# A fused transformer block on one core: attention probabilities of chunks 8 to 11 weighed in one run at the next group's first chunk, where chunks 8 and 9 had a run of their own

## The chip, the cores and the metric

The kernel runs on one core of a Trainium2 chip. Its time is the device time of one execution in microseconds (us), as the median of several executions.

## What is computed

The reference is one transformer block in float32 with a shift, scale and gate per batch entry: a causal attention with 16 heads of 32 and then a mixture of 32 experts with a shared expert. Only the attention matters here:

```python
B, S, D_MODEL, N_HEADS, D_K = 8, 1024, 512, 16, 32
q, k, v = proj(w_q, b_q), proj(w_k, b_k), proj(w_v, b_v)
scores = einsum('bhqd,bhkd->bhqk', q, k) / sqrt(D_K)
scores = where(causal, scores, -inf)
attn = softmax(scores, axis=-1)
out = einsum('bhqk,bhkd->bqhd', attn, v)
x = x + ga * (out @ w_o.T + b_o)
h = layernorm(x) * (1 + cb) + sb
x = x + gb * (routed experts(h) + shared expert(h))
```

## The kernel before, in words

The program has four stages on one core, one after the other: the projections to queries, keys and values (lines with the tile prefix qkv_), the attention (att_), the output projection with the shared expert (ffn_) and the routed experts (exp_). Work is handed between the engines by semaphores, and the order of each engine's work is written out by hand.

**Groups and chunks.** The attention works on 32 groups (GROUPS), each of one batch entry and four heads (GH = 4). The keys lie on the partitions: a chunk is one tile of 128 keys against one half of 512 queries, for the four heads. A group has 12 chunks, in the order of the list `chunks`. Chunks 0 to 3 belong to the first half of the queries, 4 to 11 to the second. A chunk on the causal diagonal has fewer queries: chunks 8 and 9 have 512 a head, chunk 10 has 256 and chunk 11 has 128. `heads_each` puts several narrow heads into one bank, so a chunk is 4, 2 or 1 "problems" (chunk 10 has two, chunk 11 one).

**The loop of TensorE** is `step` in `tensor`, once per group `prev` (the next group is `cur`). For each problem it computes the transposed scores into one of three banks `ps_p` (line 1385; on the diagonal line 1388 adds a mask), and lets ScalarE know. Between them it computes pieces of the plain scores of the next group into four banks `ps_s` (`scores`, line 1303; `TILES` says how many behind each problem; from chunk 9 on they are those of the group after next). VectorE takes the row maxima from these (`maxima`, lines 247 and 253) so that the softmax can subtract them: at chunk 9 they are turned (line 1367), VectorE writes `m_hi` and `m_lo` (lines 266 and 268), and SyncE copies both into a row each of the next group's queries (`load_maxima`, line 236). TensorE waits for those two copies (`m_in`) before the next group's chunk 0.

**Exponentials.** ScalarE turns each problem's bank into probabilities in a tile `pt` (lines 1165 and 1168). There are 9 tiles for 12 chunks (`PT`), so a chunk's first exponential waits in `tile_free` until the tile's former user has been weighed (`pv_done`) and its sum taken. GpSimd adds chunks' tiles together for the sums of the softmax (`join`, lines 1097 to 1104), and TensorE adds the rest with ones (`total`, line 1360; in the last group `last_total`, line 1337).

**Weighing** (`weigh`, line 1329) multiplies a chunk's probabilities with the values: for each of the four heads a matmul with 128x32 weights, whose result takes 32 of the 128 partitions of the bank `ps_o`. In the trace each of these matmuls is two instructions, so a chunk is 8. `step` weighs two chunks at a time, after the last problem of each even chunk c:

```python
                    group = prev if c else older(prev)
                    if group and c % 2 == 0:
                        weigh(group, (c - 2) % NC)
                        weigh(group, (c - 1) % NC)
```

So chunks 8 and 9 are weighed at chunk 10, and chunks 10 and 11 at chunk 0 of the next group. ScalarE takes the finished half out of the bank (`take`, line 1122) at chunk 1.

**The end of the stage.** In the last group there are no plain scores. Its sums are computed chunk by chunk with ones; behind the loop come the sums and then the weighing of chunks 10 and 11. ScalarE meanwhile has the last exponential, five copies of weights (lines 1180 and 1185), with `take_total(end, 1)` (line 1128) ahead of the last of them, and then `take(end, NC - 1)`. The next stage's first transpose on TensorE (line 2209) waits for `t_free`, which that `take_total` gives; its ScalarE work waits behind `take`. SyncE and GpSimd start their part of the next stage once the last chunk has been weighed.

Of the kernel before, what the change touches and what calls it, by code (L numbers as in the profile page):

```python
# [857 lines left out]
def attention_programs(nc, x, qk_dram, v_dram, o_dram, inv_dram, mod_dram, woT, bo, gateT, sh_upT, bridge, before):  # L858
# [7 lines left out]
    with ExitStack() as ctx:  # L866
# [32 lines left out]
        NC = len(chunks)  # L899


        def span(c):
            qh, kt = chunks[c]
            return max(kt * P - qh * UNIT, 0)
# [23 lines left out]
        LATER = (3, 11)  # L928


        STORED_BY = 5
        assert all(PT[c] < 6 for c in range(STORED_BY))

# [38 lines left out]
        def tile(c):  # L972
            return pt[PT[c]]
# [24 lines left out]
        def older(prev):  # L998

            if isinstance(prev.g, int) and prev.g == 0:  # L1000
                return None
            return Group(prev.g - 1, (prev.slot - 1) % SLOT, None)
# [111 lines left out]
        def scalar(act):  # L1114
# [15 lines left out]
            def tile_free(group, c):  # L1130

                user, back = user_before(c)
                if back > group.g:
                    return
                act.wait_ge(pv_done, CREDIT + NC * (group.g - back) + user + 1)
                owner = group.g - back
                if owner == GROUPS - 1 and user in HALF[1]:
                    act.wait_ge(add_done, CREDIT + ADDED + 1)
                elif owner == GROUPS - 1 or owner == GROUPS - 2 and user in ALONE:
                    act.wait_ge(sum_done, CREDIT + QH * owner + chunks[user][0] + 1)  # L1140
                elif user in INTO:
                    act.wait_ge(add_done, CREDIT + NJ * (group.g - back) + JOINS.index(user) + 1)
                elif user == 4:
                    act.wait_ge(add_done, CREDIT + NJ * (group.g - back) + JOINS.index(5) + 1)
                else:
                    act.wait_ge(sum_done, CREDIT + QH * (group.g - back) + chunks[user][0] + 1)

            def step(cur, prev):
                for n, (c, h) in enumerate(problems):
# [8 lines left out]
                    if h == 0:  # L1158
                        tile_free(prev, c)
                    if h == 0 and c == STORED_BY and prev.g == 0:  # L1160
                        for stored, count in before.stored:
# [119 lines left out]
        def tensor(pe):  # L1281
# [40 lines left out]
            def weigh(group, c):  # L1322
                qh, kt = chunks[c]
                col = span(c)
                if kt == 0:
                    pe.wait_ge(o_free, CREDIT + QH * group.g + qh)
                pe.wait_ge(exp_done, CREDIT + NPROB * group.g + ENDED[c])
                for h in range(GH):
                    last = pe.matmul(ps_o[h * HD:(h + 1) * HD, col:UNIT], vs[group.slot][:, kt, h * HD:(h + 1) * HD],  # L1329
                                     tile(c)[:, h, col:UNIT], start=kt == 0, stop=c in ENDS)  # L1330
                last.then_inc(pv_done, 1)
# [9 lines left out]
            def last_total(qh, todo):  # L1341

                for c in todo:
                    pe.wait_ge(exp_done, CREDIT + NPROB * (GROUPS - 1) + ENDED[c])
                    if c == HALF[qh][0]:
                        bank_free("sum", GROUPS - 1, qh)
                    last = part(c, bank("sum", GROUPS - 1, qh))
                    if c == 5:
                        last.then_inc(add_done, 1)
                    if c in ENDS:  # L1350
                        last.then_inc(sum_done, 1)
# [17 lines left out]
            def step(cur, prev):  # L1369
                for n, (c, h) in enumerate(problems):  # L1370
# [26 lines left out]
                    if n + 1 < ENDED[c]:  # L1397
                        continue
                    group = prev if c else older(prev)
                    if group and c % 2 == 0:  # L1400
                        weigh(group, (c - 2) % NC)
                        weigh(group, (c - 1) % NC)
                    if cur and c == TOTAL_AT[0]:
                        total(prev, 0)
                    if cur and c == TOTAL_AT[1] and older(prev):
# [13 lines left out]
            scores(Group(1, 1, 0), 0, EARLY)  # L1419
            pe.wait_ge(before.ev_done, CREDIT + before.tiles)  # L1420
            steps(step)(pe)
            end = Group(GROUPS - 1, (GROUPS - 1) % SLOT, None)
            last_total(1, (NC - 2, NC - 1))
            weigh(end, NC - 2)
            weigh(end, NC - 1)

        return Programs(sync, gpsimd, scalar, vector, tensor)


# [925 lines left out]
```

## Time and profile before

| what | us |
|---|---|
| median of 3 runs (lowest, highest) | 3001.86 (2996.71, 3007.34) |
| the profiled execution's own time | 3024.03 |
| its span, first to last instruction | 3022.3 |
| TensorE (PE) busy | 2920.5 (97%) |
| VectorE (DVE), ScalarE (ACT), GpSimd (POOL) busy | 2117.6, 1343.0, 1837.8 |
| mean granted TensorE clock | 0.984 of full |

All times of the trace are counted from the start of the span. PE is matmuls, PEld the loads of their weights, SPq the DMA queue of SyncE. A matmul's row gives its start and its whole latency; neighbours overlap, so what one adds to the path is the distance between two starts, not the duration. A timeline merges like instructions that follow each other (x16) and says in brackets how long the engine was idle before, and what it then got.

### The profile page before, as it was taken

The page shows a single profiled execution, that of the slowest core. Times are in us where ns is not written, and L with a number is a line of the kernel's source. Part 1 is how long each engine was busy: PE and PEld are TensorE (multiplying, and loading weights), DVE is VectorE, ACT ScalarE, POOL GpSimd, SP SyncE. Part 2 cuts the span into 40 slices and gives each one's busy share as a digit, 9 for nine tenths or more (in the row PEclk, how much of TensorE's full clock was granted, in tenths as well). Part 3 has the DMA queues.
Part 4 walks back from the last instruction along what each step waited for, and adds up shares of the span by engine and source line. Part 5 has one row for each costly group of instructions (what it writes and reads, how often), then busy time and mean ns, then how long its engine had stood idle before and what let it go on. Part 6 is the DMA issues. An engine that isn't in the chain of part 4 may idle for free. (4 is left out here: it accounts for less than half of the span.)

```text
span 3022.3 us, 49806 instructions
## 1 busy us (share of the span) xinstructions
PE 2920.5 (97%) x16480; PEld 2169.3 (72%) x16480; DVE 2117.6 (70%) x5344; ACT 1343.0 (44%) x2436; POOL 1837.8 (61%) x1077
## 2 busy tenths in 40 slices
PE   8999999999999999999999899999999999989997
PEld 5788888766666666666666577787877888768775
DVE  6555555677777777777777586787878888856764
ACT  2222222166666666666666532323332233226764
POOL 1332223278788887888878146567665776655664
PEclk9999999999999999999999999999999999999998
DMA  7555555755655566555664332233323332248996
GB/s 257 195 203 193 184 180 177 236 113 134 134 128 115 121 134 135 122 115 125 135 138 121 125 112 74 81 102 109 98 74 109 101 99 81 74 132 213 234 235 119
DMA packets 281948, 420.53 MB, mean 139 GB/s; under 512 B 48463, under 2 KB 132687, under 8 KB 281742
## 3 DMA queue, kind: packets, MB, share of 16 engines
q1 hardware_dynamic: 259214, 384.22, 44.7%
q0 software_dynamic: 22528, 33.72, 5.8%
q8 instruction: 109, 1.79, 0.2%
q14 instruction: 97, 0.79, 0.1%
HBM read 263.38 MB, written 153.01 MB: 138 GB/s over the span
## 5 line engine op out<-in xcount | busy, mean ns | idle before, releaser
L1165 ACT ACTIVATE att_pt<-att_ps_p 128x512 f32<-128x512 f32 (+1 forms) x1024 | 524.8, 586 | 142.6 <-PE att_ps_p L1388 118.2
L247 DVE CUSTOM_DVE_ANT_0 att_ps_s<-att_ps_s,att_causal 128x512 f32<-128x512 f32 (+1 forms) x992 | 470.0, 503 | 137.2 <-PE att_ps_s L1303 136.9
L1385 PE MATMUL att_ps_p<-att_qs,att_ks 98*128 98x512 f32 (+3 forms) x1536 | 505.3, 369 | 8.2 <-ACT att_pt L1165 7.8
L1303 PE MATMUL att_ps_s<-att_ks,att_qs 96*128 96x512 f32 x1488 | 508.2, 370 | 2.2 <-DVE att_lower L253 0.6
L253 DVE TENSOR_REDUCE att_lower<-att_ps_s 128x1 f32<-128x512 f32 x496 | 339.9, 685 | 115.1 <-PE att_ps_s L1303 115.0
L1104 POOL TENSOR_TENSOR att_gathered<-att_gathered,att_pt 128x2048 f32<-128x2048 f32 (+1 forms) x92 | 388.4, 4222 | 41.2 <-ACT att_pt L1165 36.4
L1385 PEld LDWEIGHTS att_ps_p<-att_qs,att_ks 98*128 98x128 f32 x1536 | 272.2, 191 | 152.7 <-issue 106.0
L1097 POOL TENSOR_TENSOR att_pt<-att_pt 128x1024 f32<-128x1024 f32 (+2 forms) x153 | 331.3, 2165 | 70.2 <-PE att_ps_o L1329 52.5
L1911 POOL DMA_INDIRECT slot_info<-ffn_info,ffn_slot x256 | 276.1, 1078 | 113.5 <-issue 78.7
L1303 PEld LDWEIGHTS att_ps_s<-att_ks,att_qs 96*128 96x128 f32 x1488 | 275.2, 191 | 68.5 <-DVE att_rowmax L247 22.1
L577 POOL TENSOR_TENSOR qkv_x<-qkv_x,qkv_mod 128x512 f32<-128x512 f32 x60 | 83.5, 1392 | 368.1 <-DVE qkv_x L671 368.1
L1329 PE MATMUL att_ps_o<-att_pt,att_vs 128*32 128x512 f32 (+3 forms) x3072 | 288.2, 493 | 0.0
L2190 PE MATMUL ffn_ps_m<-ffn_dn_hi,ffn_a_hi 128*128 128x512 f32 x512 | 208.5, 407 | 2.4 <-ACT ffn_relu L1964 2.1
L1872 POOL TENSOR_TENSOR ffn_h<-ffn_h,ffn_mod 128x512 f32<-128x512 f32 x45 | 70.8, 1572 | 221.1 <-DVE ffn_h L2024 221.1
L2190 PE MATMUL ffn_ps_m<-ffn_dn_hi,ffn_a_lo 128*128 128x512 f32 x512 | 202.8, 396 | 0.0
L2190 PE MATMUL ffn_ps_m<-ffn_dn_lo,ffn_a_hi 128*128 128x512 f32 x512 | 202.7, 396 | 0.0
L2190 PE MATMUL ffn_ps_m<-ffn_hT_hi,ffn_up_hi_first 128*128 128x512 f32 x512 | 201.8, 394 | 0.0
L840 PE MATMUL qkv_ps_m<-qkv_hT_hi,qkv_w_hi 128*128 128x512 f32 x512 | 200.0, 391 | 1.4 <-DVE qkv_hT_lo L676 1.4
L2190 PE MATMUL ffn_ps_m<-ffn_hT_hi,ffn_up_lo_first 128*128 128x512 f32 x512 | 199.9, 390 | 0.0
L2190 PE MATMUL ffn_ps_m<-ffn_hT_lo,ffn_up_hi_first 128*128 128x512 f32 x512 | 199.9, 390 | 0.0
L840 PE MATMUL qkv_ps_m<-qkv_hT_hi,qkv_w_lo 128*128 128x512 f32 x512 | 199.4, 389 | 0.0
L840 PE MATMUL qkv_ps_m<-qkv_hT_lo,qkv_w_hi 128*128 128x512 f32 x512 | 199.4, 389 | 0.0
(311 smaller groups left out, 6558.4 us busy)
## 6 DMA issues: line engine op xcount, KB each, us to landing
att_qs<-qk_parts SPq DMA_DIRECT2D x96, 512.0 KB, 6.8
att_ks<-qk_parts SPq DMA_DIRECT2D x96, 512.0 KB, 12.8
qk_parts<-qkv_out_hi SPq DMA_DIRECT2D x128, 256.0 KB, 2.2
qk_parts<-qkv_out_lo SPq DMA_DIRECT2D x128, 256.0 KB, 2.4
qkv_x<-x SPq DMA_DIRECT2D x16, 1024.0 KB, 5.4
v_rows<-qkv_out_v SPq DMA_DIRECT2D x64, 256.0 KB, 2.3
att_vs<-v_rows SPq DMA_DIRECT2D x32, 512.0 KB, 16.0
o_parts<-att_o SPq DMA_DIRECT2D x64, 256.0 KB, 7.5
```

What stands on the lines that cost most here:

```text
L247: dve.tensor_tensor_reduce(part, part, self.causal[:, UNIT - (c1 - c0):UNIT], scale=1.0, scalar=MASKED, op0=ALU.add, op1=ALU.max, accum_ou ...
L253: dve.reduce_max(under[:, low:low + 1], part, axis=AX.X).then_inc(self.max_done, 1)
L577: pool.tensor_tensor(xt, xt, mod[:, 1, :], ALU.mult).then_inc(mul_done, 1)
L840: last = pe.matmul(ps_m[n % BANKS][:, :], w_part[:, k, (n % NG) * P:(n % NG + 1) * P], h_part[:, k, :], start=k == 0 and a + c == 0, stop= ...
L1097: pool.tensor_tensor(into, into, tile(c)[:, :, col:UNIT], ALU.add).then_inc(add_done, 1)
L1104: pool.tensor_tensor(into, into, tile(c)[:, :, col:UNIT], ALU.add).then_inc(add_done, 1)
L1165: act.activation(tile(c)[:, h, col:UNIT], ps_p[(NPROB * prev.g + n) % NP][:, col:UNIT], ACT.Exp, scale=float(HD) ** -0.5).then_inc(exp_don ...
L1303: pe.matmul(bank("s", cur.g, i)[:, 0:c1 - c0], qs[cur.slot][0:STACK, h, t * P:(t + 1) * P], ks[cur.slot][0:STACK, h, c0:c1], start=True, s ...
L1329: last = pe.matmul(ps_o[h * HD:(h + 1) * HD, col:UNIT], vs[group.slot][:, kt, h * HD:(h + 1) * HD], tile(c)[:, h, col:UNIT], start=kt == 0 ...
L1385: last = pe.matmul(part[:, i * (UNIT - col):(i + 1) * (UNIT - col)], ks[prev.slot][:, h + i, kt * P:(kt + 1) * P], qs[prev.slot][:, h + i, ...
L1911: pool.indirect_dma_start(info_dram[:, :], bass.IndirectOffsetOnAxis(slot[half][:, j:j + 1].bitcast(U32), 0), info[half][:, j, :], None, b ...
L2190: last = pe.matmul(bank, a[m], c[n], start=i + j == 0, stop=i + 1 == len(pairs) and j == 2)
```

## The change

A table says which chunks are weighed behind which. The order of weighing stays 0 to 11. Only chunks 8 and 9 move: from behind chunk 10 of their own group to behind chunk 0 of the next, just ahead of 10 and 11. In the last group they move behind the sums at the end.

```diff
+        WEIGHED_AT = {0: (8, 9, 10, 11), 2: (0, 1), 4: (2, 3), 6: (4, 5), 8: (6, 7)}
...
                     group = prev if c else older(prev)
-                    if group and c % 2 == 0:
-                        weigh(group, (c - 2) % NC)
-                        weigh(group, (c - 1) % NC)
+                    if group and c in WEIGHED_AT:
+                        for weighed in WEIGHED_AT[c]:
+                            weigh(group, weighed)
...
             last_total(1, (NC - 2, NC - 1))
-            weigh(end, NC - 2)
-            weigh(end, NC - 1)
+            for weighed in WEIGHED_AT[0]:
+                weigh(end, weighed)
```

Lines behind the new table are one further down in the changed kernel (1329 is 1330, and so on).

**The boundary of two groups on TensorE.** These are its instructions from the end of chunk 10 to the start of chunk 0, before. A shape is rows of the result by columns; 32x512 is one head of a chunk in `weigh`. What a row waits for stands behind it (att_m_in1 are the copies of the maxima).

```order
L1388 MATMUL att_ps_p<-att_mask_k,att_ident_r 128x2x128
L1303 MATMUL att_ps_s<-att_ks,att_qs 128x128 [waits att_max]
L1329 MATMUL att_ps_o<-att_pt,att_vs 32x512 [waits att_exp]
L1329 MATMUL att_ps_o<-att_pt,att_vs 32x512 x3
L1329 MATMUL att_ps_o<-att_pt,att_vs 32x512 [waits att_exp]
L1329 MATMUL att_ps_o<-att_pt,att_vs 32x512 x3
L1385 MATMUL att_ps_p<-att_qs,att_ks 128x128 [waits att_exp]
L1385 MATMUL att_ps_p<-att_qs,att_ks 128x128 x3
L1388 MATMUL att_ps_p<-att_mask_k,att_ident_r 128x512
L1303 MATMUL att_ps_s<-att_ks,att_qs 128x512 [waits att_max] x2
L1385 MATMUL att_ps_p<-att_qs,att_ks 128x512 [waits att_exp,att_v_in1,att_m_in1]
```

And the same stretch of the changed kernel:

```order
L1389 MATMUL att_ps_p<-att_mask_k,att_ident_r 128x2x128
L1304 MATMUL att_ps_s<-att_ks,att_qs 128x128 [waits att_max]
L1386 MATMUL att_ps_p<-att_qs,att_ks 128x128 [waits att_exp]
L1386 MATMUL att_ps_p<-att_qs,att_ks 128x128 x3
L1389 MATMUL att_ps_p<-att_mask_k,att_ident_r 128x512
L1304 MATMUL att_ps_s<-att_ks,att_qs 128x512 [waits att_max] x2
L1386 MATMUL att_ps_p<-att_qs,att_ks 128x512 [waits att_exp,att_v_in1,att_m_in1]
```

The 8 matmuls of chunks 8 and 9 are gone from between chunks 10 and 11; they now stand at the end of chunk 0, whose last rows in the changed kernel are these:

```order
L1304 MATMUL att_ps_s<-att_ks,att_qs 128x512 [waits att_max]
L1330 MATMUL att_ps_o<-att_pt,att_vs 32x512 [waits att_exp]
L1330 MATMUL att_ps_o<-att_pt,att_vs 32x512 x3
L1330 MATMUL att_ps_o<-att_pt,att_vs 32x512 [waits att_exp]
L1330 MATMUL att_ps_o<-att_pt,att_vs 32x512 x3
L1330 MATMUL att_ps_o<-att_pt,att_vs 32x256 [waits att_exp]
L1330 MATMUL att_ps_o<-att_pt,att_vs 32x256 x3
L1330 MATMUL att_ps_o<-att_pt,att_vs 32x128 [waits att_exp]
L1330 MATMUL att_ps_o<-att_pt,att_vs 32x128 x3
L1386 MATMUL att_ps_p<-att_qs,att_ks 128x384 [waits att_exp]
```

The number of matmuls is the same, and there is one run of weighing fewer per boundary. The order of the other engines' instructions is unchanged.

## Rows read from the trace of the kernel before

**Rows 1.** Busy time by stage, the stretch of the attention; PE, PEld, DVE, ACT, POOL, clock, DMA.

```profile
617.00:1716.00 1099.00, 1089.26 (x7680) 688.86 (x7680) 794.77 (x2656) 686.46 (x1339) 861.17 (x276) 1.00 0.54 123
```

**Rows 2.** Timeline of PE, end of chunk 10 to chunk 1: start, us, instruction.

```profile
1013.91 0.23 PE L1303 MATMUL att_ps_s<-att_ks,att_qs 96*128 96x128 f32 x1
1014.06 1.92 PE L1329 MATMUL att_ps_o<-att_pt,att_vs 128*32 128x512 f32 x16
1015.92 0.66 PE L1385 MATMUL att_ps_p<-att_qs,att_ks 98*128 98x128 f32 x4
...
1019.20 0.45 PE L1303 MATMUL att_ps_s<-att_ks,att_qs 96*128 96x512 f32 x1
1019.58 0.86 PE L1329 MATMUL att_ps_o<-att_pt,att_vs 128*32 128x256 f32 x16
1020.37 0.44 PE L1385 MATMUL att_ps_p<-att_qs,att_ks 98*128 98x384 f32 x1
```

**Rows 3.** Timeline of PE, the run of chunks 0 and 1 (512 and 384 columns).

```profile
1023.86 1.71 PE L1329 MATMUL att_ps_o<-att_pt,att_vs 128*32 128x512 f32 x16
1025.50 0.66 PE L1385 MATMUL att_ps_p<-att_qs,att_ks 98*128 98x128 f32 x4
```

**Rows 4.** Timeline of PEld, around chunk 11 and chunk 0.

```profile
1013.79 0.19 PEld L1303 LDWEIGHTS att_ps_s<-att_ks,att_qs 96*128 96x128 f32 x1
...
1015.92 0.52 PEld L1385 LDWEIGHTS att_ps_p<-att_qs,att_ks 98*128 98x128 f32 x4 [0.84 <-issue]
1016.36 0.19 PEld L1388 LDWEIGHTS att_ps_p<-att_mask_k,att_ident_r 128*128 128x128 f32 x1
...
1016.94 0.19 PEld L1385 LDWEIGHTS att_ps_p<-att_qs,att_ks 98*128 98x128 f32 x1
```

**Rows 5.** Timeline of DVE, first piece of chunk 11.

```profile
1017.14 0.69 DVE L253 TENSOR_REDUCE att_lower<-att_ps_s 128x1 f32<-128x512 f32 x1 [2.24 <-PE att_ps_s L1303]
```

**Rows 6.** Timeline of ACT, chunk 11's exponential and chunk 1's first.

```profile
1016.98 0.60 ACT L1168 ACTIVATE att_pt<-att_ps_p 128x512 f32<-128x512 f32 x1 [2.23 <-PE att_ps_p L1388]
...
1020.99 0.49 ACT L1165 ACTIVATE att_pt<-att_ps_p 128x384 f32<-128x384 f32 x1 [0.95 <-PE att_ps_p L1388]
```

**Rows 7.** Timeline of POOL, the sums of chunks 7 and 8.

```profile
1006.92 8.15 POOL L1104 TENSOR_TENSOR att_gathered<-att_gathered,att_pt 128x1536 f32<-128x1536 f32 x2 [1.18 <-ACT att_pt L1165]
```

**Rows 8.** Timeline of SPq, the copy of m_lo.

```profile
1012.22 0.59 SPq L236 DMA_DIRECT2D att_qs<-att_m_lo  x1
```

**Rows 9.** The instructions of line 236 from 617 to 1700 us: duration min/median/max in ns.

```profile
L236 SPq DMA_DIRECT2D att_qs<-att_m_lo x31: 587/590/1179, 636.1 to 1661.9; - x31
...
DMA to landing us min/median/max: 2.1/2.1/2.9
```

**Rows 10.** Timeline of all engines, end of the last group.

```profile
1709.48 2.63 PE L1329 MATMUL att_ps_o<-att_pt,att_vs 128*32 128x512 f32 x16
...
1713.77 0.66 PE L1385 MATMUL att_ps_p<-att_qs,att_ks 98*128 98x128 f32 x4
...
1714.83 0.60 ACT L1168 ACTIVATE att_pt<-att_ps_p 128x512 f32<-128x512 f32 x1 [4.64 <-PE att_ps_p L1388]
...
1715.73 0.83 PE L1329 MATMUL att_ps_o<-att_pt,att_vs 128*32 128x256 f32 x16
...
1718.37 0.58 ACT L1128 ACTIVATE att_total<-att_ps_s 128x512 f32<-128x512 f32 x1
...
1719.00 1.09 PE L2209 MATMUL ffn_ps_t<-all_ident,ffn_h 128*128 128x128 f32 x8 [2.45 <-ACT att_total L1128]
```

**Rows 11.** Busy time in stretches around the end of the attention; the clock third from last.

```profile
1708.00:1710.00 2.00, 2.00 (x11) 1.46 (x14) 1.97 (x5) 1.80 (x4) 0.00 (x0) 0.50 0.03 8
...
1722.00:1725.00 3.00, 1.94 (x8) 1.57 (x8) 1.53 (x3) 1.19 (x2) 0.00 (x0) 0.50 1.06 309
```

**Rows 12.** Timeline of PEld, two of the four waits for VectorE in chunk 4.

```profile
1028.02 0.19 PEld L1303 LDWEIGHTS att_ps_s<-att_ks,att_qs 96*128 96x128 f32 x1 [0.23 <-DVE att_rowmax L247]
1028.51 0.19 PEld L1303 LDWEIGHTS att_ps_s<-att_ks,att_qs 96*128 96x128 f32 x1 [0.30 <-DVE att_rowmax L247]
```

## The prediction

> **What bounds the kernel now.** I read the busy time by stage first. The attention takes 1099 us of the 3022.3 us span; in it TensorE is busy for 1089 us at the full clock, which is its 2.4 GHz level, and VectorE, ScalarE and GpSimd for 795, 686 and 861 us [rows 1]. So TensorE is the path there, and a change of the order counts by what it does to the distances between TensorE's starts. Next I read TensorE's timeline from chunk 10 to chunk 1. The run of chunks 8 and 9 starts at 1014.06 and chunk 11's first matmul at 1015.92, 1.86 us later. The run of chunks 10 and 11 starts at 1019.58, and chunk 1 follows 0.79 us later [rows 2]. Then the weight loads (what the array may load ahead), and last the other engines at the same place, for what the pause in the scores gives them.
>
> **What a run costs beyond its columns.** Count columns a head: chunks 8 and 9 have 1024 and took 1.86 us, chunks 0 and 1 have 896 and took 1.64 us, chunks 10 and 11 have 384 and took 0.79 us [rows 2, 3]. From 384 to 896 columns it is 0.85 us for 512, from 896 to 1024 it is 0.22 us for 128. So the columns cost 0.85 us per 512 in every run, 1.71 us for chunks 8 and 9, and every run has 0.15 us on top, whatever its length. That is a price of leaving the run. Entering costs too: the score matmul ahead of the run starts at 1013.91 and the run 0.15 us later.
>
> **The change part by part.**
>
> *Chunks 8 and 9 leave chunk 10 (31 boundaries of 32 groups).* From the score matmul at 1013.91 to the load of chunk 11's mask at 1016.36 it is 2.45 us now [rows 2, 4]. Without the run only chunk 11's four loads lie between. They go at one per 0.11 us (1015.92 to 1016.36 for four), and the first can start when the score matmul before it starts, 0.11 to 0.12 us after that one's own load at 1013.79 [rows 4]. So it takes 0.44 us, and chunk 11 and everything behind it comes 2.01 us earlier.
>
> *They join the run behind chunk 0.* That run exists, with its entry and exit. By the line above it grows by the columns alone, 1.71 us. Net per boundary: 2.01 - 1.71 = 0.30 us. The rows stand for 31 boundaries alike; the run at chunk 10 takes 1.85 or 1.86 us at each. Bounds: at least the 0.15 us of the exit is saved, if the gap at the entry is only a late record; at most 0.42 us, if the loads of chunk 11 can go one score matmul (0.12 us) further ahead. I take 0.30: it comes from the nearest rows, those of the place itself. 31 x 0.30 = **9.3 us**.
>
> The Trainium skill (TensorEngine Tiling (Array Packing), Key Properties) says that a change of the tiling mode drains the array, and TensorE: Matmul & The Clock Gate (Single matmul latency) puts the part of a matmul that a drain exposes at 166 ns. By these pages, as an estimate, two changes fewer are worth 0.33 us a boundary, 10.3 us in all, against 9.3 by the rows.
>
> *Other engines, during the 2.01 us.* Nothing is issued more or less; what goes is a pause. VectorE was idle for 2.24 us before chunk 11's first piece [rows 5] and ScalarE for 2.23 us before chunk 11's exponential [rows 6]. Both idle times end by TensorE and shrink to 0.23 and 0.22 us, so these engines still wait for TensorE, and what follows up to the end of chunk 0 keeps its spacing. Cost: nothing, with a cover of 0.2 us. Chunk 1's tile is that of chunk 8, which is now weighed later. Its exponential waits for that weighing, but chunk 1's matmuls stand behind the run on TensorE anyway, and ScalarE was idle for 0.95 us there, waiting for them [rows 6]. The other thing it waits for, GpSimd's sum of chunk 8, is over at 1006.92 + 8.15 = 1015.07, 5.9 us before that exponential [rows 7]. The loads of the group after next wait for chunk 11's weighing, whose time in the group does not move; GpSimd's sums wait for the weighing of chunks 0 and 6 only.
>
> *The copies of the maxima.* SyncE issues the copy of m_lo at 1012.22, it lands 2.1 us later in the median (2.9 at most) [rows 8, 9], at 1014.3. Chunk 0's first load, which waits for it, is at 1016.94 [rows 4] and would be at 14.93 on this scale. The 2.6 us of slack become 0.6. Cost in the median copy nothing; what is behind it is a rival below.
>
> *The last group.* Here chunks 8 and 9 stand between narrow matmuls with ones on either side before and after, so no entry or exit goes. But the sums of chunks 10 and 11 come earlier. Now the weighing and the sums of 8 and 9 take from 1709.48 to 1713.77, 4.29 us [rows 10]: 3.41 for columns, 0.15 exit, the rest because the clock was at 0.50 (1.2 GHz) at first [rows 11]. With the sums alone, the slow stretch falling on them, about 2.7 us. So chunk 11, its exponential (1714.83), the queue of copies behind it and the take of the last sum (1718.37) come 1.6 us earlier. The last weighing ends where it did, near 1716.6 [rows 10]. TensorE now waits 2.45 us for that take before the next stage's first transpose at 1719.00, so the wait has room for all of it: **1.6 us**, between 0 (if ScalarE's weights or a later transfer hold it) and 1.6.
>
> **The sum.** 9.3 + 1.6 = 10.9 us. The profiled execution's own time is 3024.03 us (its span is 3022.3), which would become 3013.1. That execution lies 22 us above the median of the runs shown; the attention's share should be alike in both, so the median goes from 3001.86 to **2991.0 us**, 0.36% less. A measurement of this kernel can tell about 0.3%, 9 us, from no change. The three runs differ by 10.6 us among themselves, and the half-clock stretches between stages, as at 1722 to 1725 [rows 11], fall where they will; I add 5 us either way for that.
>
> **The rivals.**
>
> *The maxima come too late (same side, smaller).* For: the slack falls from 2.6 to 0.6 us, and the longest landing was 2.9 us [rows 9]. Against: the median is 2.1. If every copy took 2.9, it would land at 15.12 against 14.93, a wait of 0.2 us at 31 boundaries, 6.2 us. Then the change brings 10.9 - 6.2 = 4.7 us: 2997.2.
>
> *The price is per matmul, not per run (no change).* Each matmul of a run might pay for its own weights, since the load can't go ahead of the one before; then a longer run saves nothing. Against it: runs of the same 16 instructions and 1024, 896 and 384 columns lie on one line with 0.15 us over, so at most that 0.15 can be the instructions' own. Then the boundaries bring nothing and the last group's 1.6 us alone remain: 3000.3. The Trainium skill (TensorE: Matmul & The Clock Gate, Part 3, The mechanism) has such a rule: weight loads overlap running matmuls only where the row groups differ, and here all four heads use all rows.
>
> *The scores run into VectorE (slower).* The pause at chunk 10 is where VectorE empties its queue. From chunk 9 to the end of chunk 0 there are now 13 pieces without one. If VectorE's queue at chunk 11 is more than the 0.23 us of spare time longer, the four banks fill up and TensorE's loads wait, as they do four times in chunk 4, 0.2 to 0.3 us each [rows 12], about 1.0 us. At 31 boundaries: 31 x (1.0 - 0.30) - 1.6 = +20 us: 3022. It decides from a loss of 0.6 us a boundary on. Against: the 2.24 us of idle time is real in this trace and larger than the 2.01 us taken, and the long run behind chunk 0 gives the pause back.
>
> **How the numbers follow.** The forecast has 0.72, the late maxima 0.14, the price per matmul 0.08, VectorE 0.06. Within the forecast 10.9 us is just above the 9 us that count as faster, and the noise of two medians can hide it: I give 0.62 to faster and 0.10 to same. Same is then 0.10 + 0.14 + 0.08 less 0.01, which goes to slower for a disturbed measurement: 0.31; slower is 0.07. The low end is the upper bound's gain, 0.42 x 31 + 1.6 = 14.6 us, 2987.2, and 2 us of the luck with the clock: 2985. The high end takes in the lower bound, 0.15 x 31 + 1.6 = 6.3 us (2995.6), and the two milder rivals: 3001.
>
> **What would show it.** In the changed profile: between chunk 10's last score and chunk 11's mask load 0.44 us; one run of 32 instructions behind chunk 0 that is 2.50 us long to chunk 1's first matmul; a group shorter by 0.3 us; VectorE's and ScalarE's idle times at chunk 11 at 0.2 us instead of 2.2; the attention's stretch 9 us shorter; the take of the last sum 1.6 us nearer to the last group's chunk 10. A releaser "DMA att_qs<-att_m_lo" before chunk 0 would show the first rival, loads of the scores that wait for att_rowmax or att_lower in chunk 0 the third. The prediction is wrong if the longer run takes more than 2.6 us, or if chunk 11 starts later than 0.3 us behind chunk 10's last score.

## The result, and the profile after

| | us |
|---|---|
| before, median of 20 runs (lowest, highest) | 3005.75 (2994.76, 3017.53) |
| changed, median of 20 runs (lowest, highest) | 2994.36 (2984.10, 3007.72) |
| ratio, with its 95% interval | 0.9960 [0.9948, 0.9972] |
| forecast and its range | 2991.0 (2985.0 to 3001.0), ratio 0.9964 |
| changed, the profiled execution: own time, span, mean granted clock | 2997.19, 2995.4, 0.988 |

The change saves 11.4 us, 0.4%, which is more than the 0.3% that a measurement of this kernel can tell from nothing.

The page of the changed kernel, busy time of each engine over the span; the numbers of instructions are those of before:

```profile
PE 2899.0 (97%) x16480; PEld 2159.9 (72%) x16480; DVE 2120.9 (71%) x5344; ACT 1340.9 (45%) x2436; POOL 1837.7 (61%) x1077
```

Busy time by stage, the attention of the changed kernel, with the columns of [rows 1]:

```profile
614.00:1703.00 1089.00, 1078.79 (x7652) 688.07 (x7655) 794.58 (x2655) 685.53 (x1339) 860.69 (x276) 1.00 0.55 125
```

The stretch is 10 us shorter than the one in [rows 1]. VectorE's, ScalarE's and GpSimd's busy times are the same within 1 us, and TensorE's fell with the stretch: TensorE still is the path.

TensorE from chunk 11 to chunk 1 in the changed kernel; it answers to [rows 2]:

```profile
1007.56 0.23 PE L1304 MATMUL att_ps_s<-att_ks,att_qs 96*128 96x128 f32 x1
1007.62 0.61 PE L1386 MATMUL att_ps_p<-att_qs,att_ks 98*128 98x128 f32 x4
...
1010.85 0.45 PE L1304 MATMUL att_ps_s<-att_ks,att_qs 96*128 96x512 f32 x1
1011.23 2.57 PE L1330 MATMUL att_ps_o<-att_pt,att_vs 128*32 128x512 f32 x32
1013.74 0.45 PE L1386 MATMUL att_ps_p<-att_qs,att_ks 98*128 98x384 f32 x1
```

The weight loads at the same place; they answer to [rows 4]:

```profile
1007.56 0.53 PEld L1386 LDWEIGHTS att_ps_p<-att_qs,att_ks 98*128 98x128 f32 x4
1008.01 0.19 PEld L1389 LDWEIGHTS att_ps_p<-att_mask_k,att_ident_r 128*128 128x128 f32 x1
```

Chunk 11's matmuls now start 0.06 us behind chunk 10's last score matmul, and its mask load 0.45 us behind it (1007.56 to 1008.01), where it was 2.45 us. The run of 32 instructions takes 2.51 us up to chunk 1's first matmul (1011.23 to 1013.74), where 10 and 11 alone took 0.79. So 2.00 us went and 1.72 came.

VectorE's first piece of chunk 11 and its first of chunk 1, which answer to [rows 5]:

```profile
1008.79 0.69 DVE L253 TENSOR_REDUCE att_lower<-att_ps_s 128x1 f32<-128x512 f32 x1 [0.23 <-PE att_ps_s L1304]
...
1014.67 0.57 DVE L247 CUSTOM_DVE_ANT_0 att_ps_s<-att_ps_s,att_causal 128x384 f32<-128x384 f32 x1 [2.16 <-PE att_ps_s L1304]
```

ScalarE, chunk 11's exponential and chunk 1's first, as in [rows 6]:

```profile
1008.64 0.60 ACT L1169 ACTIVATE att_pt<-att_ps_p 128x512 f32<-128x512 f32 x1 [0.22 <-PE att_ps_p L1389]
...
1014.36 0.49 ACT L1166 ACTIVATE att_pt<-att_ps_p 128x384 f32<-128x384 f32 x1 [2.68 <-PE att_ps_p L1389]
```

The pause that both engines had at chunk 11 stands at chunk 1 now. 0.23 and 0.22 us are left of it at chunk 11, so both still wait for TensorE there and not the other way round.

The waits of the changed kernel from 614 to 1690 us, those of chunk 0's loads and matmuls for the copies of the maxima (us in total, times, the longest in us):

```profile
PEld att_ps_p L1386 <- DMA att_qs<-att_m_lo: 2.0, 5, 0.8
PE att_ps_p L1386 <- DMA att_qs<-att_m_lo: 0.4, 1, 0.4
```

And line 236 of the changed kernel, from 614 to 1703 us, with the columns of [rows 9]:

```profile
L236 SPq DMA_DIRECT2D att_qs<-att_m_lo x31: 590/590/1438, 632.8 to 1650.8; - x31
...
DMA to landing us min/median/max: 2.1/2.1/3.5
```

This wait did not exist before. It comes at 5 of the 31 boundaries.

The end of the last group in the changed kernel, which answers to [rows 10]:

```profile
1697.64 3.54 PE L1338 MATMUL att_ps_s<-att_pt,att_ones 128*32 128x512 f32 x16
...
1701.11 0.66 PE L1386 MATMUL att_ps_p<-att_qs,att_ks 98*128 98x128 f32 x4
...
1703.07 2.55 PE L1330 MATMUL att_ps_o<-att_pt,att_vs 128*32 128x512 f32 x32
...
1705.71 0.58 ACT L1129 ACTIVATE att_total<-att_ps_s 128x512 f32<-128x512 f32 x1
...
1706.35 1.09 PE L2210 MATMUL ffn_ps_t<-all_ident,ffn_h 128*128 128x128 f32 x8 [0.73 <-ACT att_total L1129]
```

TensorE's wait for the take fell from 2.45 to 0.73 us.

**A ruler for the rest.** TensorE turns the row maxima once per group (line 1368, 1367 before), at a fixed place of the order. The distance from one turn to the next is a group's length; I call its median over the 30 distances between these turns the period. Each of the 30 holds one boundary; the 31st, to the last group, comes behind the last turn. It is 34.19 us before and 33.89 us after. All tables below are distances on TensorE's timeline. The last turn of before stands at 1660.71, that of the changed kernel at 1649.62.

**The account.** The 30 distances take 1025.78 us before and 1017.98 after: 7.8 us less. 30 x 0.30 would be 9.0; the 1.2 us that are missing stand in six distances that are 0.07 to 0.66 us over the period, and five of these, 1.13 us together, are those with the late maxima (the 0.66 is that with the wait of 0.8). From the last turn to the next stage's first transpose it is 58.29 us before and 56.73 after, 1.6 us less; about 0.2 of that is the last boundary, and the rest the last group. That makes 9.4 us for the whole change.

The two spans differ by more, 26.9 us. Ahead of these distances stands one from the turn for the first group, with no boundary in it: 38.66 us before, with 10 us at the half clock, and 34.73 after, with none. And behind the attention, where the change touches nothing, the rest of the span is 1303.3 us before and 1289.0 after. The profiled execution of before spent 98 us at the half clock in all and that of the changed kernel 71 us. The 27 us between them are worth 13.5 us at most, so some 4 us of the difference stay unexplained. The total at the half clock varies from execution to execution: in the profiles of the first four kernels below, which differ as little from these two, it is 44 to 69 us.

### The profile page after: what moved, and what is told of

Its sections match the earlier page's. It is cut to its first block and busy times, and to the rows that moved or that the text cites. A ratio compares the mean times of both kernels' runs of the same rounds, so it can differ in the third digit from the quotient of the medians.

```text
span 2995.4 us, 49806 instructions
## 1 busy us (share of the span) xinstructions
PE 2899.0 (97%) x16480; PEld 2159.9 (72%) x16480; DVE 2120.9 (71%) x5344; ACT 1340.9 (45%) x2436; POOL 1837.7 (61%) x1077
## 5 line engine op out<-in xcount | busy, mean ns | idle before, releaser
L1330 PE MATMUL att_ps_o<-att_pt,att_vs 128*32 128x512 f32 (+3 forms) x3072 | 280.9, 491 | 0.0
```

## The experiments

Eleven are edits of the changed kernel and one is that kernel again; lines of diffs are against it. They ran in three sets, each on one chip beside its own runs of the kernel before, whose medians were 3006.19, 3040.05 and 2993.35 us. So only ratios are compared across sets, and above all the periods, which agree within 0.02 us for the same order of work (33.89 and 33.91 in the two profiles of the changed kernel, 33.90 for its boundaries alone). The second set has no profile of the changed kernel; its periods are held against 33.89.

**1. The two parts of the change, each alone.** The tail alone: the last group as changed, the boundaries as before.

```diff
-        WEIGHED_AT = {0: (8, 9, 10, 11), 2: (0, 1), 4: (2, 3), 6: (4, 5), 8: (6, 7)}
+        WEIGHED_AT = {0: (10, 11), 2: (0, 1), 4: (2, 3), 6: (4, 5), 8: (6, 7), 10: (8, 9)}
...
-                    if group and c in WEIGHED_AT:
+                    if group and c in WEIGHED_AT and (cur or c != 10):
...
-            for weighed in WEIGHED_AT[0]:
+            for weighed in (8, 9, 10, 11):
```

> The last group alone is changed (chunks 8 and 9 weighed behind the last sums); the other 31 boundaries are as before. Theory (a run costs its entry and exit, 0.30 us, and the last group gives 1.6 us by the earlier take of the last sum): a group's period stays 34.19 us, the first transpose of the next stage comes 1.6 us earlier against the last group's chunk 8, time 1.6 us below before, within noise. Rival (the gain is some other effect of the last group): most of the 11 us are already there.

Measured: 3005.36 us, ratio 0.9997 [0.9977, 1.0016], period 34.18. The wait before the transpose is 0.73 us, as in the changed kernel.

The boundaries alone: the changed table, and the last group as before.

```diff
+                    if not cur and c == 10:
+                        weigh(prev, 8)
+                        weigh(prev, 9)
...
-            for weighed in WEIGHED_AT[0]:
+            for weighed in (10, 11):
```

> All boundaries changed, the last group as before. Theory: period of a group 33.89 us against 34.19, the wait for the take of the last sum back at some 2.4 us, time 7.5 us below before (9.3 less about 2 us for late copies of the maxima). Rival (the last group makes most of it): under 3 us below before.

Measured: 2998.20 us, ratio 0.9971 [0.9949, 0.9994], period 33.90. The first transpose of the next stage, here and then with the tail alone:

```profile
1707.38 1.97 PE L2213 MATMUL ffn_ps_t<-all_ident,ffn_h 128*128 128x128 f32 x8 [2.44 <-ACT att_total L1129]
```

```profile
1712.17 1.09 PE L2210 MATMUL ffn_ps_t<-all_ident,ffn_h 128*128 128x128 f32 x8 [0.73 <-ACT att_total L1129]
```

So the period belongs to the boundaries, and the wait at the end to the tail. The tail's 1.6 us are 0.05% and can't be told in the times; they rest on the trace alone.

**2. Moved but not merged.** Chunks 8 and 9 leave chunk 10, but go behind chunk 11 as a run of their own.

```diff
-        WEIGHED_AT = {0: (8, 9, 10, 11), 2: (0, 1), 4: (2, 3), 6: (4, 5), 8: (6, 7)}
+        WEIGHED_AT = {0: (10, 11), 2: (0, 1), 4: (2, 3), 6: (4, 5), 8: (6, 7), 11: (8, 9)}
...
-                    if group and c in WEIGHED_AT:
+                    if group and c in WEIGHED_AT and (cur or c != 11):
...
-            for weighed in WEIGHED_AT[0]:
+            for weighed in (8, 9, 10, 11):
```

> Chunks 8 and 9 are weighed later, behind chunk 11, but in a run of their own; 10 and 11 behind chunk 0 as before. As many runs as before. Theory (price per run): period 34.15 to 34.25 us, no wait for the copies of the maxima, time as before less the 1.6 us of the last group. Rival (what helps is that the pause in the scores comes later, or that chunk 11 follows chunk 10 without a pause): period 33.9 us, 9 us below before.

Measured: 3001.26 us, ratio 0.9985 [0.9961, 1.0008], period 34.22. The move alone brings nothing. No load waits for the maxima here, since the run of 8 and 9 stands ahead of chunk 0 as it did before.

**3. One score matmul inside the long run.** The run stays behind chunk 0, but the piece of plain scores that stood ahead of it now stands between chunks 9 and 10.

```diff
+                group_before = older(prev)
...
-                    if cur and c < TURN:
+                    if cur and c < TURN and not (group_before and n + 1 == ENDED[0]):
...
                         for weighed in WEIGHED_AT[c]:
+                            if cur and weighed == 10:
+                                scores(cur, *pieces_at(n))
                             weigh(group, weighed)
```

> As the changed kernel, but one full-width score matmul of 512 columns (the last piece of chunk 0) stands between chunks 9 and 10 inside the long run. Theory (leaving and entering the narrow shape costs 0.25 to 0.30 us): period 34.15 to 34.2 us, all of the boundaries' gain gone. Rival (the price is the wait for exponentials or the instruction queue at the start of a run, or it lies in the matmuls themselves): period stays at 33.9 us.

Measured: 2999.06 us, ratio 0.9996 [0.9974, 1.0017], period 34.19. TensorE at this place:

```profile
1013.29 0.22 PE L1390 MATMUL att_ps_p<-att_mask_k,att_ident_r 128*128 128x128 f32 x1
1013.44 1.92 PE L1330 MATMUL att_ps_o<-att_pt,att_vs 128*32 128x512 f32 x16
1015.30 0.50 PE L1304 MATMUL att_ps_s<-att_ks,att_qs 96*128 96x512 f32 x1
1015.73 0.86 PE L1330 MATMUL att_ps_o<-att_pt,att_vs 128*32 128x256 f32 x16
1016.52 0.44 PE L1387 MATMUL att_ps_p<-att_qs,att_ks 98*128 98x384 f32 x1
```

The two pieces take 1.86 and 0.79 us again, as in [rows 2]. The load of the score piece between them is put down to VectorE:

```profile
1014.33 0.14 DVE L247 DVE_READ_ACCUMULATOR2_ANT att_rowmax<- 128x1 f32 x1
1015.29 0.19 PEld L1304 LDWEIGHTS att_ps_s<-att_ks,att_qs 96*128 96x128 f32 x1 [0.84 <-DVE att_rowmax L247]
```

But VectorE was done 0.8 us earlier, at 1014.47, so a wait for VectorE is not what costs here. Every matmul is there that the changed kernel has, the weighing is as late, and the whole gain of the period is gone. What costs is the change between matmuls whose result takes 32 partitions and those whose result takes 128, there and back. Experiments 2 and 3 together leave neither the later weighing nor the number of matmuls as a cause.

**4. Does a further run cost what a missing one saves?** Chunks 4 and 5 are weighed in two runs, behind chunks 5 and 6.

```diff
-        WEIGHED_AT = {0: (8, 9, 10, 11), 2: (0, 1), 4: (2, 3), 6: (4, 5), 8: (6, 7)}
+        WEIGHED_AT = {0: (8, 9, 10, 11), 2: (0, 1), 4: (2, 3), 5: (4,), 6: (5,), 8: (6, 7)}
```

> The changed kernel with chunk 4 weighed behind chunk 5 and chunk 5 behind chunk 6, so one run of weighing more per group (32 in all), with the same matmuls. Theory (price per run): period of a group 34.15 to 34.25 us against 33.89, time some 9 to 10 us above the changed kernel. Rival (the price belongs to this boundary, where nothing loaded ahead): period 33.9 us.

Measured: 3028.56 us, ratio 0.9947 [0.9924, 0.9970], period 33.77. A miss: a further run, and a group that is 0.12 us shorter. First the price; TensorE at the first of the two runs:

```profile
999.83 1.06 PE L1330 MATMUL att_ps_o<-att_pt,att_vs 128*32 128x512 f32 x8
1000.83 0.50 PE L1386 MATMUL att_ps_p<-att_qs,att_ks 98*128 98x512 f32 x1
```

1.00 us for 512 columns, 0.15 over their 0.85: the exit price holds, and the second run takes 1.00 as well, so the two take 0.15 us more than the one did (1.85). What paid for it stands in the changed kernel, which has no run between chunks 5 and 6. Its loads there:

```profile
1027.53 0.19 PEld L1386 LDWEIGHTS att_ps_p<-att_qs,att_ks 98*128 98x128 f32 x1 [0.58 <-ACT att_pt L1166]
```

and its matmuls:

```profile
1026.96 0.39 PE L1304 MATMUL att_ps_s<-att_ks,att_qs 96*128 96x512 f32 x1
1027.53 0.50 PE L1386 MATMUL att_ps_p<-att_qs,att_ks 98*128 98x512 f32 x1 [0.18 <-ACT att_pt L1166]
```

Chunks 5 and 6 are eight exponentials in a row, and ScalarE also has a sum and a half of the output to take there. It falls behind, the three banks are full, and TensorE waits once a group: 0.57 us between these starts. A run in that place does the weighing in the time in which TensorE would wait. Outside the runs, chunks 5 and 6 take 4.25 us instead of 4.51, the entry to the new run included. The exit costs 0.15 and the rest saves 0.26. So the price of a run is one thing, and what a pause at its place is worth to the other engines another.

**5. Merging at chunk 4 and at chunk 8.** The same step as the change, at the two other places where it can be done.

```diff
-        WEIGHED_AT = {0: (8, 9, 10, 11), 2: (0, 1), 4: (2, 3), 6: (4, 5), 8: (6, 7)}
+        WEIGHED_AT = {0: (8, 9, 10, 11), 4: (0, 1, 2, 3), 6: (4, 5), 8: (6, 7)}
```

> The changed kernel with chunks 0 to 3 in one run behind chunk 4, one run fewer. Price per run alone: period 33.59 us. But the pause taken here is longer (some 1.9 us) than VectorE's idle time behind it (1.50 us at chunk 3), and TensorE waits for VectorE four times in chunk 4 already. Theory: the saved 0.30 us is eaten by about 0.4 us of such waits, period 33.9 to 34.0 us. Rival (VectorE's queue doesn't matter): 33.6 us.

Measured: 3029.35 us, ratio 0.9954 [0.9931, 0.9977], period 33.75, between the theory and its rival.

```diff
-        WEIGHED_AT = {0: (8, 9, 10, 11), 2: (0, 1), 4: (2, 3), 6: (4, 5), 8: (6, 7)}
+        WEIGHED_AT = {0: (8, 9, 10, 11), 2: (0, 1), 4: (2, 3), 8: (4, 5, 6, 7)}
```

> The changed kernel with chunks 4 to 7 in one run behind chunk 8, one run fewer. The pause taken is some 2.0 us; VectorE idles 1.89 us and ScalarE 1.79 us behind it at chunk 7. Theory: 0.30 us saved, 0.1 to 0.2 us of new waits for these two: period 33.65 to 33.8 us, 3 to 7 us below the changed kernel. Rival (no limit by the other engines): 33.59 us; rival (both queues fill up in chunks 7 and 8): above 33.9 us.

Measured: 3024.23 us, ratio 0.9938 [0.9901, 0.9974], period 33.61. Here the rival without a limit was right. The expectation took VectorE's idle time behind the run at chunk 4 for the one that matters; that behind the run at chunk 6, which goes, is longer than the pause:

```profile
1032.57 0.70 DVE L247 CUSTOM_DVE_ANT_0 att_ps_s<-att_ps_s,att_causal 128x512 f32<-128x512 f32 x1 [2.13 <-PE att_ps_s L1304]
```

At chunk 8 nearly the full price comes out, 0.28 us a group; at chunk 4 half of it, 0.14. The loads of plain scores that wait for VectorE, from 700 to 1600 us, in the changed kernel:

```profile
PEld att_ps_s L1304 <- DVE att_rowmax L247: 18.8, 80, 0.3
PEld att_ps_s L1304 <- DVE att_lower L253: 13.0, 55, 0.2
```

and with the merge at chunk 4:

```profile
PEld att_ps_s L1304 <- DVE att_rowmax L247: 23.4, 105, 0.3
PEld att_ps_s L1304 <- DVE att_lower L253: 13.0, 53, 0.2
```

One more such wait per group, 0.18 us each. VectorE was already behind in chunk 4 [rows 12], and the pause that the merge takes away is the one ahead of it.

**6. The merge at chunk 4 with the score pieces spread.** Chunk 4 had six pieces behind its four problems and chunk 6 four; two move from the one to the other.

```diff
-        WEIGHED_AT = {0: (8, 9, 10, 11), 2: (0, 1), 4: (2, 3), 6: (4, 5), 8: (6, 7)}
+        WEIGHED_AT = {0: (8, 9, 10, 11), 4: (0, 1, 2, 3), 6: (4, 5), 8: (6, 7)}
...
-        TILES = {0: [2, 1, 1, 1], 1: [2, 1, 1, 1], 2: [2, 1], 3: [2], 4: [2, 1, 2, 1], 5: [2, 1, 1, 1], 6: [1, 1, 1, 1],
+        TILES = {0: [2, 1, 1, 1], 1: [2, 1, 1, 1], 2: [2, 1], 3: [2], 4: [1, 1, 1, 1], 5: [2, 1, 1, 1], 6: [2, 1, 2, 1],
```

> As merge_c4, and two pieces of the plain scores are moved from chunk 4 (6 to 4) to chunk 6 (4 to 6), so that VectorE has 14 pieces instead of 16 in the long stretch from chunk 1 to chunk 4. Theory: two pieces are about 1.1 us of VectorE's work, so its waits in chunk 4 go: period 33.3 to 33.6 us, 9 to 18 us below the changed kernel. Rival (the waits of chunk 4 are not for VectorE's queue, or come back in chunk 6): 33.9 us or more.

Measured: 3000.81 us, ratio 0.9863 [0.9828, 0.9898], period 33.15, somewhat better than either theory. The waits now:

```profile
PEld att_ps_s L1304 <- DVE att_rowmax L247: 6.4, 40, 0.2
PEld att_ps_s L1304 <- DVE att_lower L253: 5.0, 27, 0.2
```

**7. The spread alone, and the change once more.** The spread on the table of the kernel before:

```diff
-        WEIGHED_AT = {0: (8, 9, 10, 11), 2: (0, 1), 4: (2, 3), 6: (4, 5), 8: (6, 7)}
+        WEIGHED_AT = {0: (10, 11), 2: (0, 1), 4: (2, 3), 6: (4, 5), 8: (6, 7), 10: (8, 9)}
...
-        TILES = {0: [2, 1, 1, 1], 1: [2, 1, 1, 1], 2: [2, 1], 3: [2], 4: [2, 1, 2, 1], 5: [2, 1, 1, 1], 6: [1, 1, 1, 1],
+        TILES = {0: [2, 1, 1, 1], 1: [2, 1, 1, 1], 2: [2, 1], 3: [2], 4: [1, 1, 1, 1], 5: [2, 1, 1, 1], 6: [2, 1, 2, 1],
...
-            for weighed in WEIGHED_AT[0]:
+            for weighed in (10, 11):
```

> The kernel before, all runs of weighing as there, with two pieces of the plain scores moved from chunk 4 to chunk 6. Theory (TensorE's waits for VectorE in chunk 4 cost about 0.6 us a group, beside the price of a run): period 33.6 us against 34.19, about 18 us below before, and the waits for att_rowmax and att_lower in chunk 4 gone. Rival (the pieces bring it only with the runs merged): period above 34.0 us.

Measured: 2970.55 us, ratio 0.9925 [0.9911, 0.9940], period 33.69. These two lines of waits had been 18.2 and 12.6 us in the kernel before; here they are:

```profile
PEld att_ps_s L1304 <- DVE att_rowmax L247: 4.3, 26, 0.2
PEld att_ps_s L1304 <- DVE att_lower L253: 0.2, 1, 0.2
```

26.3 us less over 26 periods is 1.0 us of the loads' waits per group; the period fell by 0.5. The rest of these waits, by that, was hidden behind matmuls that were still running. Of the 0.74 us a group in experiment 6 the spread is thus 0.50 and the merge at chunk 4 the other 0.24, where it had brought 0.14 without the spread.

The changed kernel without an edit, on the same chip:

> The changed kernel once more, on the chip of the three kernels below, to compare them with it. Expected as before: period of a group 33.89 us, 0.4% below the kernel before.

Measured: 2979.95 us, ratio 0.9956 [0.9941, 0.9971], period 33.91.

**8. Three runs a group.** All merges and the spread together.

```diff
-        WEIGHED_AT = {0: (8, 9, 10, 11), 2: (0, 1), 4: (2, 3), 6: (4, 5), 8: (6, 7)}
+        WEIGHED_AT = {0: (8, 9, 10, 11), 4: (0, 1, 2, 3), 8: (4, 5, 6, 7)}
...
+        TILES = {0: [2, 1, 1, 1], 1: [2, 1, 1, 1], 2: [2, 1], 3: [2], 4: [1, 1, 1, 1], 5: [2, 1, 1, 1], 6: [2, 1, 2, 1],
```

> Three runs a group (0 to 3 behind chunk 4, 4 to 7 behind chunk 8, 8 to 11 behind the next chunk 0), with the two pieces moved to chunk 6. If all adds up: 33.15 less the 0.28 us of merge_c8, period 32.87 us, 1.4% below before. Rival: chunks 5 to 8 now have 21 pieces without a pause, some 11.5 us of VectorE's work in 9.3 us, more than four banks can hold, and the waits come back there: period 33.2 to 33.6 us.

Measured: 2958.72 us, ratio 0.9886 [0.9867, 0.9904], period 33.22, as the rival said. The parts do not add up to 32.87 here, and the waits for VectorE are back:

```profile
PEld att_ps_s L1304 <- DVE att_lower L253: 18.0, 82, 0.2
PEld att_ps_s L1304 <- DVE att_rowmax L247: 12.8, 55, 0.3
```

Without the pause at chunk 6, chunks 5 to 8 have the crowd of pieces that chunk 4 had. So one of the two pieces goes on to chunk 10, which has only two pieces and no run any more:

```diff
-        WEIGHED_AT = {0: (8, 9, 10, 11), 2: (0, 1), 4: (2, 3), 6: (4, 5), 8: (6, 7)}
+        WEIGHED_AT = {0: (8, 9, 10, 11), 4: (0, 1, 2, 3), 8: (4, 5, 6, 7)}
...
-        TILES = {0: [2, 1, 1, 1], 1: [2, 1, 1, 1], 2: [2, 1], 3: [2], 4: [2, 1, 2, 1], 5: [2, 1, 1, 1], 6: [1, 1, 1, 1],
-                 7: [2, 1, 1, 1], 8: [1, 1, 1, 2], 9: [1, 1, 1, 1], 10: [1, 1], 11: [2]}
+        TILES = {0: [2, 1, 1, 1], 1: [2, 1, 1, 1], 2: [2, 1], 3: [2], 4: [1, 1, 1, 1], 5: [2, 1, 1, 1], 6: [2, 1, 1, 1],
+                 7: [2, 1, 1, 1], 8: [1, 1, 1, 2], 9: [1, 1, 1, 1], 10: [1, 2], 11: [2]}
```

> As three_runs, but of the two pieces one goes to chunk 6 and one to chunk 10, so chunks 5 to 8 have 20 pieces and chunks 9 to 0 have 14. If VectorE's queue is what limits both stretches: period 0.1 to 0.4 us below three_runs. Rival: the stretch from chunk 9 had only 0.23 us of VectorE's time to spare, and 0.5 us more there shows as new waits in chunk 0: period above three_runs.

Measured: 2946.18 us, ratio 0.9844 [0.9827, 0.9860], period 32.80, 0.42 below three runs. Now the parts add up: three runs fewer at 0.30 us and the spread at 0.50 make 1.40, and the period is 1.39 us below that of the kernel before. The waits:

```profile
PEld att_ps_s L1304 <- DVE att_rowmax L247: 5.3, 30, 0.2
PEld att_ps_s L1304 <- DVE att_lower L253: 0.9, 5, 0.2
```

and the run behind chunk 0, which keeps its 2.50 us:

```profile
1005.50 2.58 PE L1330 MATMUL att_ps_o<-att_pt,att_vs 128*32 128x512 f32 x32
1008.00 0.45 PE L1386 MATMUL att_ps_p<-att_qs,att_ks 98*128 98x384 f32 x1
```

This version beats both kernels: 47 us below the kernel before and 34 us below the changed one on the same chip.

The periods side by side:

| kernel | runs that return to the 128-wide shape | pieces | period, us |
|---|---|---|---|
| before; tail alone | 6 | as before | 34.19; 34.18 |
| moved, not merged | 6 | as before | 34.22 |
| one matmul between | 6 | one moved | 34.19 |
| changed (two profiles); boundaries alone | 5 | as before | 33.89, 33.91; 33.90 |
| split at 5 | 6 | as before | 33.77 |
| merged at 4 | 4 | as before | 33.75 |
| merged at 8 | 4 | as before | 33.61 |
| before, spread | 6 | spread | 33.69 |
| merged at 4, spread | 4 | spread | 33.15 |
| three runs, spread | 3 | spread | 33.22 |
| three runs, spread further | 3 | spread further | 32.80 |

## Why the prediction was right

**The price of a run: right, in size and kind.** The step "2.01 - 1.71 = 0.30 us" measured 2.00 - 1.72 = 0.28 at the place itself and 0.30 in the period. The long run took 2.51 us against 2.50 predicted, the mask load came 0.45 us behind the score matmul against 0.44. What the working drew from a line through three runs (0.85 us per 512 columns, 0.15 us on top of each) also held for a run of 512 columns (1.00 us) and for one of 1408 (2.50 us). And most of it is gone where no change of shape follows. In the changed kernel the run of chunks 2 and 3, 384 columns, is followed by the sums, which are 32 partitions wide too:

```profile
1022.71 0.86 PE L1330 MATMUL att_ps_o<-att_pt,att_vs 128*32 128x256 f32 x16
1023.38 1.04 PE L1361 MATMUL att_ps_s<-att_gathered,att_ones 128*32 128x512 f32 x8
```

0.67 us, where the run of 10 and 11 with as many columns took 0.79 [rows 2]: 0.12 of the 0.15 is paid on return to the 128-wide shape alone. That is what the Trainium skill (TensorEngine Tiling (Array Packing), Key Properties) says, a change of the tiling mode drains the array; the runs agree in that each change of shape costs, and put it at 0.30 us for there and back, against the 0.33 us that the prediction estimated from the pages. No run shows the draining itself. What the rows do show is that no weights are loaded ahead across the change: chunk 11's first load starts with its matmul behind the run, at 1015.92 [rows 2, 4], and 0.06 us ahead of it where the run is gone (1007.56 and 1007.62). How much of the price is the one and how much the other stays open.

**No extra cost elsewhere: right.** VectorE's and ScalarE's idle times of 0.23 and 0.22 us are the predicted ones to the hundredth. The cover of 0.2 us held: from 700 to 1600 us the waits for VectorE are 18.8 and 13.0 us (80 and 55 times) against 18.2 and 12.6 (78 and 53 times) before, and the shorter groups put 0.2 of a group more into these 900 us.

**The copies of the maxima: the one step that fell short.** "The 2.6 us of slack become 0.6. Cost in the median copy nothing" is right, and the mean is not the median. The forecast left the slow copies to a rival; they are a part of the forecast. Four of the five late loads waited 0.25 to 0.38 us and one 0.84; the copies took up to 1.44 us to issue instead of 0.59, or up to 3.5 us to land instead of 2.1. The distances are 1.1 us longer for it in all, far from the rival's 6.2 us. They are most of what the trace's 9.4 us lack to 10.9. With chunks 8 and 9 ahead of chunk 0 (experiment 2) no such wait occurs. Why some copies are slow was not tried. But they are not slow at random: in all fourteen traces, the kernel before included, every copy of `m_lo` that landed more than 2.5 us behind its issue is one of groups 4 to 6, 14 to 16, 24 and 25.

**The last group: right, with the half clock in another place.** The take of the last sum came 1.6 us nearer to the last turn, and the wait shrank by 1.72 us. But "with the sums alone about 2.7 us" measured 3.47 (1697.64 to 1701.11), since the half clock lay on nearly all of them. That the take came nearer all the same has two other reasons. Up to the sums the changed kernel was 0.75 us quicker (48.02 us behind the last turn, 48.77 before): 0.23 of it is there before the last group's chunk 9 and belongs to the last boundary, which the prediction counts under the 9.3, and the rest comes where the clock of before had already fallen, from 1707.6 on, with 1.9 us to go to the weighing of chunk 8. In the profile with the tail alone no half clock lies in this stretch, and the sums of chunk 10 take:

```profile
1705.08 1.92 PE L1338 MATMUL att_ps_s<-att_pt,att_ones 128*32 128x512 f32 x16
1706.93 0.66 PE L1386 MATMUL att_ps_p<-att_qs,att_ks 98*128 98x128 f32 x4
```

1.85 us (1705.08 to 1706.93). Before, the weighing of 8 and 9 stood ahead of them, 1.71 us by the prediction's line. So the step is worth 1.7 us at the full clock, by this estimate, and the wait shrank by as much, since that weighing now stands inside it.

**The price per matmul, the rival of no change: refuted.** In experiment 3 the same 32 instructions cost 0.30 us more when one score matmul stands between them. By the rule that the prediction quoted from the Trainium skill (TensorE: Matmul & The Clock Gate, Part 3, The mechanism) loads don't overlap running matmuls where the row groups are the same. Between wide matmuls this trace shows otherwise: chunk 11's four loads begin at 1007.56, with the score matmul of 0.23 us that is to run before them, and both use 96 or more of the 128 rows. Whatever of the rule holds in the runs of weighing is inside the 0.85 us per 512 columns and gave no price per run.

**The scores run into VectorE, the slower rival: not here, but real.** It is what halved the merge at chunk 4 and took 0.35 us a group from three runs. Its condition, an idle time smaller than the pause that is taken, was the right one to ask about; [rows 5] answered it for chunk 10, and [rows 12] would have answered it for chunk 4.

**The number.** 2991.0 stood against 2994.36, with 3001.86 as the base, which turned out 3.9 us low (3005.75 over 20 runs). The predicted saving was 10.9 us; the times give 11.4 [about 8.4 to 15.6 by the interval], the trace 9.4. That the time lies so near the forecast is in part luck: the interval is 7 us wide, the base 3.9 us off, and the trace 1.5 us short of the forecast.

## What to carry to other kernels

Count how often TensorE's timeline changes between matmuls with narrow results and full ones, and price each visit at its exit and entry (0.30 us here), not by its matmuls. Merge two visits where the other engines' idle time at the removed one is larger than the pause that goes: there the full price came out, at chunk 10 and at chunk 8, and at chunk 4 half of it. Look next at what that pause had been hiding: moving two small pieces of work from a crowded place to an emptier one brought more (0.50 us a group, 0.75% in the time) than the merge itself (0.30 us, 0.4%), and a run split at a place where TensorE waits anyway more than paid for itself.

## What the runs showed that was not expected

- A further change of shape can make the kernel faster: in experiment 4 TensorE waited for ScalarE once a group, and a run of 1.00 us laid there took 0.26 us away at a price of 0.15 for its exit.
- SyncE's copy of `m_lo`, 0.59 us to issue at most boundaries, takes up to 1.44 us at some, and its landing up to 3.5 us instead of 2.1. With 0.6 us of slack over the median they cost 1.1 us in the whole attention. It is the same few groups in every kernel.
- Executions of nearly the same kernel spent 44 to 102 us at the half clock in their profiles, in different stretches. A difference of two spans (26.9 us here) says little about a change of 10 us; the period says it to 0.02 us.
- The medians of the kernel before differed by 1.6% between chips (2993.35 to 3040.05 us), four times the effect of the change, while the period of the changed order of work was 33.89 us beside the first result, 33.90 in the first set and 33.91 in the third. The chips differ behind the attention: from the next stage's first transpose to the end it is 1279 to 1293 us in the profiles of the first set, 1311 to 1335 in the second and 1270 to 1275 in the third.
